# Second halves of three units' down products in three rounded passes, at the end of a recurrent-gated mixture-of-experts kernel

## Chip, cores, metric

The kernel runs on one core of a Trainium2 chip. The metric is the device time of one execution in microseconds, the median of the runs timed.

## What is computed

The input `x` is (32, 32, 128) float32. A tanh recurrence runs over 32 steps, its output goes through an RMS norm and a mixture of 16 experts with 4 chosen for each token, and `x`, the recurrence's output and the experts' sum are added. Cut to what matters:

```python
xw = jnp.einsum('ntd,dh->nth', x, Wx) + b
next_h = jnp.tanh(xw_t + prev_h @ Wh)          # 32 steps
...
xn = xf * jax.lax.rsqrt(jnp.mean(xf * xf, axis=-1, keepdims=True) + EPS) * norm_scale
vals, idx = jax.lax.top_k(xn @ wg + bg, K)     # 4 of 16
gate_full = jnp.einsum('tke,tk->te', one_hot(idx), softmax(vals))
h = jnp.einsum('th,ehd->etd', xn, w1) + b1[:, None, :]
a = jnp.minimum(h[..., ::2], LIMIT)
b = jnp.clip(h[..., 1::2], -LIMIT, LIMIT)
s = a * jax.nn.sigmoid(ALPHA * a) * (b + 1.0)
y = jnp.einsum('eti,eih->eth', s, w2) + b2[:, None, :]
t = jnp.einsum('eth,te->th', y, gate_full)     # every expert, weighted by its gate
return x + (xf + t)
```

## The kernel before

There are 1024 tokens, 8 tiles of 128. They are worked in three chunks of 2, 2 and 4 tiles. A **unit** is 512 columns of work: two experts on 256 tokens in chunks 0 and 1 (units 0 to 7 and 8 to 15), one expert on 512 tokens in chunk 2 (units 16 to 31). For each unit:

- the **up**: PE forms `a` in bank psA and `b` in psB (`up`, L913). Each is three rounded passes: weights and tokens are held as a high part rounded to the type float32r and a low part that is the rest (`w1_hi`, `w1_lo`, `xn_hi`, `xn_lo`), and the passes are high by high, low by high, high by low;
- ACT applies its two functions to psA (L586, L598), DVE clips psB into `lin` (L792) and multiplies the two into `act` (L810);
- the **gate product** `actg` = `act` times the gates laid out over the partitions (`gate_cols`). POOL makes it (L461), but for units 20, 22, 24, 26, 28 and 30 (`DVE_PRODUCT`), where DVE does (L816), and unit 31, where DVE makes it in two halves of 256 columns (L833);
- the **down**: PE adds `w2` times `actg` into the sum over experts. For chunk 2 the sum is two banks of 256 columns, psY (first half) and psM (second half).

The down has two forms. For units 0 to 15 and 28 to 31 it takes the float32 tensors `w2_sb` and `actg` as they are (L957, L969). For units 16 to 27 (`SPLIT`) it takes three rounded passes (L948), for which ACT makes `act_hi` (L550) and POOL `act_lo` (L470) of each `actg`, and earlier ACT `w2_hi` (L558) and POOL `w2_lo` (L477).

Each engine has its own program, written out by hand as a loop over units, with semaphores between them. The down of a unit comes six units after its up (`LAG`), and POOL's product three behind (`POOL_LAG`). After the last up PE runs the downs of units 26 and 27, then the float32 halves of units 28 to 31 into psY, then those into psM; these four units have no rounded parts. DVE adds `xT` to each finished bank (L840), and SP and ACT store the result (L344): the second bank in two halves of 64 partitions, one from each queue. What the end looks like on PE:

```python
for u in rest:            # 28, 29, 30, 31
    down_half(u, 0)       # psY
for u in rest:
    down_half(u, 1)       # psM
```

`down_half` waits for the product of its unit: `wait_product` for 28 to 30, `actg_tail` at 2 (both L833) for 31.

Of the kernel before, what the change touches and what calls it, by code (L numbers as in the profile page):

```python
# [15 lines left out]
def adaln_rnn_moe_kernel(nc, wx_x, small, bg, w1, w2, b2, out):  # L16
# [45 lines left out]
    SPLIT = list(range(FIRST, NU - 4))  # L62
    SPLIT_RUNS = [[u for u in SPLIT if u // 4 == k] for k in sorted({u // 4 for u in SPLIT})]
    W2_HIGH, W2_LOW = [13, 14, 17], [16, 17, 18]
    SPLIT_DEPTH = 3
    DVE_PRODUCT = list(range(FIRST + 4, NU, 2))

# [18 lines left out]
    with ctx:  # L86
        def sb(name, shape, dt=F32):
            return ctx.enter_context(nc.sbuf_tensor(name, shape, dt))
# [4 lines left out]
        def sem(name):  # L93
            return ctx.enter_context(nc.semaphore(name))
# [57 lines left out]
        actg = sb("actg", [P, SUM_DEPTH, W])  # L152
        act_hi = sb("act_hi", [P, SPLIT_DEPTH, W], F32R)
        act_lo = sb("act_lo", [P, SPLIT_DEPTH, W], F32R)
        w2_hi = sb("w2_hi", [P, len(SPLIT), H], F32R)
        w2_lo = sb("w2_lo", [P, len(SPLIT), H], F32R)
        yT = sb("yT", [P, NT * P])

        psA = [pb("psA0"), pb("psA1")]
        psB = [pb("psB0"), pb("psB1")]  # L160
# [53 lines left out]
        act_lo_ready = sem("act_lo_ready")  # L214
        w2_hi_ready = sem("w2_hi_ready")
        w2_lo_ready = sem("w2_lo_ready")
        yT_ready = sem("yT_ready")
        stored = sem("stored")
        dve_chain = sem("dve_chain")
# [110 lines left out]
        def at(table, v):  # L330
            return [k for k, w in enumerate(table) if w is not None and w == v]
# [53 lines left out]
        def _(pool):  # L385
# [101 lines left out]
            for v in range(NU - 1 + POOL_LAG):  # L487
                for q in at(RSTD, v - 1):
                    xn_low(pair_group(q))
                for q in at(POWER, v):  # L490
                    power_rstd(pair_group(q))
                for q in at(RSTD, v):
                    power_expo(q)
                    place_expo(q)
                for i in at(W2_LOW, v):
                    w2_low(i)
                if v >= POOL_LAG and v - POOL_LAG not in DVE_PRODUCT:
                    gate_product(v - POOL_LAG)
                for u in SPLIT:
                    if split_slot(u) == v:  # L500
                        act_low(u)
                for q in at(GATES, v - 1):
                    add_residuals(q)

        @block.scalar
        def _(acte):

            acte.dma_start(small_h[:, 0:SM], small).then_inc(small_loaded, 16)
            acte.dma_start(b2_sb[:, :], b2).then_inc(b2_loaded, 16)
            acte.wait_ge(ident_ready, 1)  # L510
            nc.scalar.activation(act[:, 0, 0:1], zeros[:, 0:1], ACT.Gelu_apprx_sigmoid)

            def tanh(t):
                acte.wait_ge(step_mm, t + 1)
                nc.scalar.activation(hT[:, (t + 1) * N:(t + 2) * N], step_psum(t), ACT.Tanh,
                                     bias=b_col[:, 0:1]).then_inc(step_done, 1)

            def w1_high(k):

                p, a = k // 2, k % 2  # L520
                pe_ = slice(2 * p, 2 * p + 2)
                acte.wait_ge(w1_loaded[2 * p // EG], 16)
                nc.scalar.activation(w1_hi[:, pe_, a, :], w1_sb[:, pe_, a, :], ACT.Copy).then_inc(w1_hi_ready, 1)

            def square(g):

                acte.wait_ge(step_done, TL * GROUP0[g + 1])
                nc.scalar.activation(sq[:, group_cols(g)], hT[:, group_cols(g, N)], ACT.Square).then_inc(sq_ready, 1)

            def scale_gates(q):  # L530
                acte.wait_ge(inv_ready, q + 1)
                for j in pair_tiles(q):
                    last = nc.scalar.activation(
                        gates_w[:, j, :].rearrange("p (a b e) -> p a b e", a=3, b=2)[:, :, 0, :],
                        gate_sum[:, j, :].rearrange("p (a e) -> p a e", a=1).to_broadcast([P, 3, E]),
                        ACT.Copy, scale=inv[:, j:j + 1])
                last.then_inc(scale_done, 1)

            def copy_gates(q):
                acte.wait_ge(gates_mm, q + 1)  # L540
                qc = slice(q * PW, (q + 1) * PW)
                nc.scalar.activation(gT[:, qc], psX[0:E, 0:PW], ACT.Copy).then_inc(gT_ready, 1)

            def act_high(u):

                i = SPLIT.index(u)
                wait_product(acte, u)
                if i >= SPLIT_DEPTH:
                    acte.wait_ge(y_mm, SPLIT[i - SPLIT_DEPTH] + 1)
                nc.scalar.activation(act_hi[:, i % SPLIT_DEPTH, :], actg[:, u % SUM_DEPTH, :],  # L550
                                     ACT.Copy).then_inc(act_hi_ready, 1)

            def w2_high(i):

                to, es = w2_run(i)
                for g in range(NG):
                    acte.wait_ge(w2_loaded[g], 16)
                nc.scalar.activation(w2_hi[:, to, :], w2_sb[:, es, :], ACT.Copy).then_inc(w2_hi_ready, 1)  # L558

            acte.wait_ge(small_loaded, 16)  # L560
            for t in range(HEAD):
                tanh(t)
                if t == TL:
                    square(0)
                elif t == HEAD - 1:
                    square(1)
                elif t >= W1_AT:
                    w1_high(2 * W1_DVE + t - W1_AT)
            acte.wait_ge(consts_ready, 1)
            for k in range(2 * W1_DVE + HEAD - 1 - W1_AT, 2 * NP):  # L570
                w1_high(k)
            for u in range(NU):
                c, e0, r = unit(u)
                for k in SPLIT:
                    if split_slot(k) == u:
                        act_high(k)
                if u == 0:
                    acte.wait_ge(b1_ready, 1)

                acte.wait_ge(a_mm, u + 1)  # L580
                for k in range(r):
                    if k == 1 and u < LAG:
                        for t in steps_at(u, 0):
                            tanh(t)
                    o = part(c, k)
                    last = nc.scalar.activation(psA[u % 2][:, o], psA[u % 2][:, o], ACT.Relu, scale=-1.0,  # L586
                                                bias=lim_b1a[:, e0 + k:e0 + k + 1])
                last.then_inc(relu_done, 1)
                if u >= LAG:
                    for t in steps_at(u, 0):  # L590
                        tanh(t)

                for q in range(1, NQ):
                    if GATES[q] + 1 == u:
                        scale_gates(q)
                acte.wait_ge(relu_done, u + 1)
                w = width(u)
                nc.scalar.activation(psA[u % 2][:, 0:w], psA[u % 2][:, 0:w], ACT.Gelu_apprx_sigmoid, scale=-1.0,  # L598
                                     bias=limit_col[:, :]).then_inc(swish_done, 1)
                for t in steps_at(u, 1):  # L600
                    tanh(t)
                if u == GATES[0]:
                    scale_gates(0)
                for q in at(GATES_T, u):
                    copy_gates(q)
                if u == LAST_T:
                    copy_gates(NQ - 1)
                for q in at(STATS, u + 1):
                    square(pair_group(q))
                for i in at(W2_HIGH, u):  # L610
                    w2_high(i)
            acte.wait_ge(yT_ready, NC + 1)
            store(acte, slice((NT - 2) * P, NT * P), slice(P // 2, P))

        @block.vector
        def _(dve):
# [163 lines left out]
            for v in range(NU):  # L780
# [38 lines left out]
                    gates_halves(q)  # L819
                if v == LAST_T + 1:  # L820
                    gates_halves(NQ - 1)
                for q in at(RSTD, v):
                    route_logits(q)
                    route_top(q)
                    route_index(q)
                    route_float(q)
                    route_hot(q)
# [4 lines left out]
            for o in pieces(u):  # L832
                nc.vector.tensor_tensor(by_pair(actg[:, u % SUM_DEPTH, o]), by_pair(act[:, u % ACT_DEPTH, o]), gate_block(u, o),  # L833
                                        ALU.mult).then_inc(actg_tail, 1)
            dve.wait_ge(xh_ready, NQ)
            for k in range(2):
                dve.wait_ge(y_done, k + 1)
# [5 lines left out]
        def _(pe):  # L843
# [117 lines left out]
            def down_half(u, k):  # L961
# [9 lines left out]
                if u == NU - 1:  # L971
                    ins.then_inc(y_done, 1)

            keep_warm(WARM_START)
            x_wx(0, 1)
            pe.wait_ge(small_loaded, 16)
# [60 lines left out]
            rest = range(SPLIT[-1] + 1, NU)  # L1037
            for u in range(NU - LAG, rest.start):
                down(u)
            for u in rest:  # L1040
                down_half(u, 0)
            for u in rest:
                down_half(u, 1)


# [29 lines left out]
```

## Time and profile before

| what | value |
|---|---|
| median of 3 runs | 103.24 us (103.24 to 103.46) |
| the profiled execution's own time | 102.98 us |
| its span, first to last instruction | 100.9 us |
| granted TensorE clock over the span | 1.00 of full speed |
| PE busy | 95.8 us, 95% of the span |
| DVE, ACT, POOL busy | 73.0, 69.5, 73.1 us |

The span is what the trace shows; the time of an execution holds some 2 us more around it. Times in rows are microseconds from the start of the span. PE is TensorE's matmuls, PEld its weight loads, DVE is VectorE, ACT ScalarE, POOL GpSimd, SP SyncE. A float32 matmul of 256 columns stands as two records, a rounded one as one. Records on one engine overlap, so the distance between two starts tells more than the length of one. `w_sb` in a row is `w1_sb` or `w2_sb`, `w_hi` and `w_lo` the parts of either.

### The profile page before, as it was taken

Reading aid. Unit: us, or ns where it says so; the run is one execution under the profiler, and the core shown is the slowest. Engines: PE = TensorE matmul, PEld = TensorE weight load, DVE = VectorE, ACT = ScalarE, POOL = GpSimd, SP = SyncE. Lnnn points to the kernel's source line nnn. Section 1 sums busy time; section 2 is a strip of 40 time slices with the busy share of each in tenths; the row PEclk is TensorE's granted clock in tenths of the full one; section 3 lists DMA queues with packets and bytes.
Section 4 is the critical chain, followed back from the end, with each engine's and each line's share of the span. In section 5 each row is a group of like instructions: output and inputs, shape, how many; then the busy total and the mean of one; then the engine's idle time right before and its main releaser. Section 6 shows DMA issues by size and latency. Waiting matters only on the chain.

```text
span 100.9 us, 1849 instructions
## 1 busy us (share of the span) xinstructions
PE 95.8 (95%) x589; PEld 82.0 (81%) x590; DVE 73.0 (72%) x187; ACT 69.5 (69%) x158; POOL 73.1 (73%) x83
## 2 busy tenths in 40 slices
PE   6999999999999999999999899999999999999970
PEld 2666678799999899999999688888878888889750
DVE  0306699689599785995879987669796977969630
ACT  3335997989685956769388668668887898996000
POOL 6001239993769993499817999999999999899400
PEclk9999999999999999999999999999999999999999
DMA  2998960017920009950499004992100000000012
GB/s 53 237 328 282 408 236 0 6 47 302 375 120 0 6 7 226 387 223 7 133 340 351 15 4 121 305 365 95 48 7 0 6 0 0 0 0 0 6 52 52
DMA packets 5001, 12.99 MB, mean 129 GB/s; under 512 B 752, under 2 KB 1792, under 8 KB 4992
## 3 DMA queue, kind: packets, MB, share of 16 engines
q1 hardware_dynamic: 4672, 12.66, 36.4%
q10 hardware_dynamic: 320, 0.21, 0.8%
q8 instruction: 5, 0.08, 0.3%
q14 instruction: 4, 0.03, 0.1%
HBM read 12.28 MB, written 0.59 MB: 128 GB/s over the span
## 4 chain that ended last, share of the span: by engine, by line
PE 31%; POOL 30%; DVE 11%; issue 10%; DMA 7%; ACT 4%; POOLq 2%; SPq 2%; DVEq 0%
POOL actg L461 15%; POOL act_lo L470 10%; PE psA L913 8%; DMA w_sb<-in_w 7%; PE psB L913 7%; PE psY L957 5%; POOL w_lo L477 3%; DVE lin L792 2%; POOLq L86 2%; PE psM L969 2%; PE psY L858 2%; PE psR L858 2%; PE psY L969 2%; PE psM L874 1%; DVE act L810 1%
## 5 line engine op out<-in xcount | busy, mean ns | idle before, releaser
L792 DVE TENSOR_SCALAR lin<-psB,one_b1b 128x256 f32<-128x256 f32 (+1 forms) x48 | 25.9, 568 | 11.2 <-PE psB L913 10.9
L586 ACT ACTIVATE psA<-psA,lim_b1a 128x256 f32<-128x256 f32 (+1 forms) x48 | 23.9, 515 | 11.6 <-PE psA L913 11.6
L461 POOL TENSOR_TENSOR actg<-act,gate_cols 128x512 f32<-128x512 f32 x25 | 31.9, 1289 | 0.0
L598 ACT ACTIVATE psA<-psA,limit_col 128x512 f32<-128x512 f32 x32 | 21.1, 659 | 0.8
L810 DVE SCALAR_TENSOR_TENSOR act<-lin,psA 128x512 f32<-128x512 f32 x26 | 17.8, 686 | 1.7 <-ACT psA L598 0.6
L913 PE MATMUL psA<-xn_hi,w_hi 128*128 128x256 f32 (+1 forms) x48 | 18.0, 376 | 0.4 <-DVE act L810 0.3
L913 PE MATMUL psB<-xn_hi,w_hi 128*128 128x256 f32 (+1 forms) x48 | 15.8, 330 | 0.0
L470 POOL TENSOR_TENSOR act_lo<-actg,act_hi 128x512 fp32r<-128x512 f32 x12 | 15.4, 1300 | 0.4 <-ACT act_hi L550 0.4
L913 PE MATMUL psB<-xn_lo,w_hi 128*128 128x256 f32 (+1 forms) x48 | 15.3, 318 | 0.0
L913 PE MATMUL psB<-xn_hi,w_lo 128*128 128x256 f32 (+1 forms) x48 | 15.3, 318 | 0.0
L913 PE MATMUL psA<-xn_hi,w_lo 128*128 128x256 f32 (+1 forms) x48 | 15.3, 319 | 0.0
L913 PE MATMUL psA<-xn_lo,w_hi 128*128 128x256 f32 (+1 forms) x48 | 15.1, 318 | 0.0
L414 POOL TENSOR_TENSOR rstd<-meansq,neg_half 128x2 f32<-128x2 f32 (+1 forms) x5 | 3.3, 655 | 11.6 <-DVE meansq L633 8.9
L422 POOL TENSOR_TENSOR expo<-euler,diff 128x6 f32<-128x6 f32 x4 | 5.3, 1329 | 8.1 <-DVE diff L687 8.1
L913 PEld LDWEIGHTS psA<-xn_hi,w_hi 128*128 128x128 f32 x48 | 9.1, 190 | 1.4 <-issue 1.2
L913 PEld LDWEIGHTS psB<-xn_hi,w_hi 128*128 128x128 f32 x48 | 9.1, 189 | 0.7
L913 PEld LDWEIGHTS psB<-xn_lo,w_hi 128*128 128x128 f32 x48 | 9.1, 189 | 0.7
L913 PEld LDWEIGHTS psB<-xn_hi,w_lo 128*128 128x128 f32 x48 | 9.1, 190 | 0.6
L913 PEld LDWEIGHTS psA<-xn_lo,w_hi 128*128 128x128 f32 x48 | 8.9, 188 | 0.7
L913 PEld LDWEIGHTS psA<-xn_hi,w_lo 128*128 128x128 f32 x48 | 9.1, 190 | 0.2
L957 PE MATMUL psY<-actg,w_sb 128*128 128x256 f32 x32 | 8.7, 395 | 0.0
L957 PE MATMUL psR<-actg,w_sb 128*128 128x256 f32 x32 | 8.2, 379 | 0.0
(112 smaller groups left out, 190.4 us busy)
## 6 DMA issues: line engine op xcount, KB each, us to landing
gate_cols<-gate_rows SPq DMA_DIRECT2D x16, 512.0 KB, 5.5
w_sb<-in_w SPq DMA_DIRECT2D x4, 512.0 KB, 7.5
w_sb<-in_w SPq DMA_DIRECT2D x4, 256.0 KB, 8.6
out<-yT SPq DMA_DIRECT2D x3, 128.0 KB, 1.7
wx_x_sb<-in_wx_x SPq DMA_DIRECT2D x1, 320.0 KB, 4.7
wx_x_sb<-in_wx_x SPq DMA_DIRECT2D x2, 128.0 KB, 2.6
small_h<-in_small ACTq DMA_DIRECT2D x1, 105.0 KB, 2.7
gate_rows<-gT SPq DMA_DIRECT2D x4, 16.0 KB, 1.5
```

The source lines that it names most:

```text
L414: nc.gpsimd.tensor_tensor(rstd[:, ts.start:ts.stop], meansq[:, ts.start:ts.stop], neg_half[:, :].to_broadcast([P, len(ts)]), ALU.pow).then ...
L422: nc.gpsimd.tensor_tensor(expo[:, tq, 1:K], euler[:, :, :], diff[:, tq, 1:K], ALU.pow).then_inc(pool_chain, 1)
L461: nc.gpsimd.tensor_tensor(by_pair(actg[:, u % SUM_DEPTH, w]), by_pair(act[:, u % ACT_DEPTH, w]), gate_block(u, w), ALU.mult).then_inc(actg ...
L470: nc.gpsimd.tensor_tensor(act_lo[:, i % SPLIT_DEPTH, :], actg[:, u % SUM_DEPTH, :], act_hi[:, i % SPLIT_DEPTH, :].bitcast(F32), ALU.subtra ...
L586: last = nc.scalar.activation(psA[u % 2][:, o], psA[u % 2][:, o], ACT.Relu, scale=-1.0, bias=lim_b1a[:, e0 + k:e0 + k + 1])
L598: nc.scalar.activation(psA[u % 2][:, 0:w], psA[u % 2][:, 0:w], ACT.Gelu_apprx_sigmoid, scale=-1.0, bias=limit_col[:, :]).then_inc(swish_do ...
L792: last = nc.vector.tensor_scalar(lin[:, v % 2, o], psB[v % 2][:, o], one_b1b[:, e0 + k:e0 + k + 1], LIMIT + 1.0, ALU.add, ALU.min)
L810: nc.vector.scalar_tensor_tensor(to, lin[:, v % 2, 0:w], 1.0 - LIMIT, psA[v % 2][:, 0:w], ALU.max, ALU.mult).then_inc(act_done, 1)
L858: nc.tensor.matmul(step_psum(t), wh_sb, hT[:, t * N:(t + 1) * N], start=False, stop=True, skip_group_check=True).then_inc(step_mm, 1)
L913: last = nc.tensor.matmul(bank[:, part(c, k)], w[:, e0 + k, a, :], x_part[:, cols(c)], start=((k, m) in first), stop=((k, m) in end))
L957: last = nc.tensor.matmul(y, w2_sb[:, e0 + k, :], actg[:, u % SUM_DEPTH, a], start=False, stop=(e0 + k == E - 1))
L969: ins = nc.tensor.matmul(y, w2_sb[:, e0, :], actg[:, u % SUM_DEPTH, o], start=False, stop=(u == NU - 1))
```

## The change

For units 28, 29 and 30 the second half of the down (256 columns, into psM) is made of three rounded passes in place of one float32 matmul. This needs:

- the high and low parts of `w2` for these three experts: one ACT copy of 384 columns behind unit 18's second function, and one DVE subtraction of 384 columns behind unit 19's product (`W2_TAIL_HIGH`, `W2_TAIL_LOW`);
- the high parts of the second halves of `actg`: three ACT copies of 256 columns after unit 31's functions (`tail_high`), in the order 28, 30, 29;
- their low parts: two POOL subtractions of 256 columns (28 and 30) after its last product, and one DVE subtraction (29) after unit 31's two products.

The parts of `actg` lie in the first six experts' place of `w1_lo`, which unit 21's up was the last to read. `yT` now lies in `sq`. PE takes the first halves in the order 28, 30, 29, 31, then nine rounded passes (`down_tail`), then unit 31's second half in float32.

```diff
+    TAIL_FIRST = SPLIT[-1] + 1
+    TAIL = [TAIL_FIRST, TAIL_FIRST + 2, TAIL_FIRST + 1]
+    TAIL_TO = slice(len(SPLIT), len(SPLIT) + len(TAIL))
+    TAIL_FROM = slice(TAIL_FIRST - FIRST, NU - 1 - FIRST)
+    W2_TAIL_HIGH, W2_TAIL_LOW = 18, 19
...
-        w2_hi = sb("w2_hi", [P, len(SPLIT), H], F32R)
-        w2_lo = sb("w2_lo", [P, len(SPLIT), H], F32R)
-        yT = sb("yT", [P, NT * P])
+        w2_hi = sb("w2_hi", [P, len(SPLIT) + len(TAIL), H], F32R)
+        w2_lo = sb("w2_lo", [P, len(SPLIT) + len(TAIL), H], F32R)
+        tail_hi = w1_lo[:, 0:len(TAIL), :, :].rearrange("p e a f -> p e (a f)")
+        tail_lo = w1_lo[:, len(TAIL):2 * len(TAIL), :, :].rearrange("p e a f -> p e (a f)")
+        yT = sq
...
@@ POOL, after the loop over units
+            for i in range(len(TAIL) - 1):
+                pool.wait_ge(tail_hi_ready, i + 1)
+                nc.gpsimd.tensor_tensor(tail_lo[:, i, :], actg[:, TAIL[i] % SUM_DEPTH, PW:W],
+                                        tail_hi[:, i, :].bitcast(F32), ALU.subtract).then_inc(tail_lo_ready, 1)
...
@@ ACT
+            def tail_high(u):
+
+                wait_product(acte, u)
+                nc.scalar.activation(tail_hi[:, TAIL.index(u), :], actg[:, u % SUM_DEPTH, PW:W],
+                                     ACT.Copy).then_inc(tail_hi_ready, 1)
...
+                if u == W2_TAIL_HIGH:
+                    nc.scalar.activation(w2_hi[:, TAIL_TO, :], w2_sb[:, TAIL_FROM, :], ACT.Copy).then_inc(w2_tail_hi, 1)
+            acte.wait_ge(b_mm, FIRST + 2 * len(TAIL))
+            for u in TAIL:
+                tail_high(u)
...
@@ DVE, in the loop, and after unit 31's two products
+                if v == W2_TAIL_LOW:
+                    dve.wait_ge(w2_tail_hi, 1)
+                    nc.vector.tensor_tensor(w2_lo[:, TAIL_TO, :], w2_sb[:, TAIL_FROM, :], w2_hi[:, TAIL_TO, :].bitcast(F32),
+                                            ALU.subtract).then_inc(w2_tail_ready, 1)
...
+            i = len(TAIL) - 1
+            dve.wait_ge(tail_hi_ready, i + 1)
+            nc.vector.tensor_tensor(tail_lo[:, i, :], actg[:, TAIL[i] % SUM_DEPTH, PW:W],
+                                    tail_hi[:, i, :].bitcast(F32), ALU.subtract).then_inc(tail_last_ready, 1)
...
@@ PE
+            def down_tail():
+
+                o, y = y_end(1)
+                pe.wait_ge(w2_tail_ready, 1)
+                for m, (w, x_part) in enumerate(((w2_hi, tail_hi), (w2_lo, tail_hi), (w2_hi, tail_lo))):
+                    for i in range(len(TAIL)):
+                        if m == 0:
+                            pe.wait_ge(tail_hi_ready, i + 1)
+                        elif m == 2 and i < len(TAIL) - 1:
+                            pe.wait_ge(tail_lo_ready, i + 1)
+                        elif m == 2:
+                            pe.wait_ge(tail_last_ready, 1)
+                        k = len(SPLIT) + TAIL[i] - TAIL_FIRST
+                        nc.tensor.matmul(y, w[:, k, :], x_part[:, i, :], start=False, stop=False)
...
-            for u in rest:
+            for u in TAIL + [NU - 1]:
                 down_half(u, 0)
-            for u in rest:
-                down_half(u, 1)
+            down_tail()
+            down_half(NU - 1, 1)
```

The end of PE's program before, from the first half of unit 28's down (`w_sb` is `w2_sb`, and the last word names the semaphore waited for):

```order
477 L969 MATMUL psY<-actg,w_sb 128x256 [waits actg_dve]
478 L969 MATMUL psY<-actg,w_sb 128x256 [waits actg_done]
479 L969 MATMUL psY<-actg,w_sb 128x256 [waits actg_dve]
480 L969 MATMUL psY<-actg,w_sb 128x256 [waits actg_tail]
481 L969 MATMUL psM<-actg,w_sb 128x256 [waits actg_dve]
482 L969 MATMUL psM<-actg,w_sb 128x256 [waits actg_done]
483 L969 MATMUL psM<-actg,w_sb 128x256 [waits actg_dve]
484 L969 MATMUL psM<-actg,w_sb 128x256 [waits actg_tail]
```

And with the change (`w_lo` here is the place that holds `tail_hi` and `tail_lo`):

```order
477 L1004 MATMUL psY<-actg,w_sb 128x256 [waits actg_dve] x2
478 L1004 MATMUL psY<-actg,w_sb 128x256 [waits actg_done]
479 L1004 MATMUL psY<-actg,w_sb 128x256 [waits actg_tail]
480 L1022 MATMUL psM<-w_lo,w_hi 128x256 [waits tail_hi_ready,w2_tail_ready]
481 L1022 MATMUL psM<-w_lo,w_hi 128x256 [waits tail_hi_ready] x2
482 L1022 MATMUL psM<-w_lo 128x256 x3
483 L1022 MATMUL psM<-w_lo,w_hi 128x256 [waits tail_lo_ready] x2
484 L1022 MATMUL psM<-w_lo,w_hi 128x256 [waits tail_last_ready]
485 L1004 MATMUL psM<-actg,w_sb 128x256 [waits actg_tail]
```

Unit 30's first half now stands ahead of unit 29's, and nine rounded matmuls with waits for new parts stand where three float32 ones did.

DVE's program around unit 19's product (row 140) with the change; before, row 142 followed row 140 at once:

```order
139 L819 TENSOR_SCALAR lin<-psB,one_b1b 128x512 [waits b_mm]
140 L837 SCALAR_TENSOR_TENSOR act<-lin,psA 128x512 [waits actg_done,swish_done,lin_done]
141 L851 TENSOR_TENSOR w_lo<-w_sb,w_hi 128x384 [waits w2_tail_hi]
142 L819 TENSOR_SCALAR lin<-psB,one_b1b 128x512 [waits b_mm]
143 L837 SCALAR_TENSOR_TENSOR psX<-lin,psA 128x512 [waits swish_done,lin_done]
```

One subtraction with both inputs in SBUF has come in ahead of unit 20's clip.

DVE's end with the change; the subtraction at 175 is new:

```order
172 L837 SCALAR_TENSOR_TENSOR act<-lin,psA 128x512 [waits actg_done,swish_done,lin_done]
173 L864 TENSOR_TENSOR actg<-act,gate_cols 128x256 [waits cols_loaded3_3,y_mm,cols_loaded2_3,act_done]
174 L864 TENSOR_TENSOR actg<-act,gate_cols 128x256
175 L868 TENSOR_TENSOR w_lo<-actg,w_lo 128x256 [waits tail_hi_ready]
176 L875 TENSOR_TENSOR sq<-wx_x_sb,psY 128x256 [waits y_done,xh_ready]
177 L875 TENSOR_TENSOR sq<-wx_x_sb,psM 128x256 [waits y_done]
```

Between unit 31's products and the two last additions DVE now has the low part of unit 29.

## Rows read from the trace of the kernel before

**Rows 1.** Busy time by stretch; the first line names the columns.

```profile
core 0: us, PE busy (x) PEld busy (x) DVE busy (x) ACT busy (x) POOL busy (x), PEclk, DMA share, GB/s
...
75.20:93.70 18.50, 18.50 (x110) 16.46 (x111) 15.02 (x23) 15.49 (x26) 18.12 (x15) 1.00 0.00 1
93.75:97.70 3.95, 3.88 (x18) 2.77 (x16) 1.63 (x3) 0.00 (x0) 0.59 (x1) 1.00 0.11 33
```

**Rows 2.** The chain that ended last, in order of time: start, us, what.

```profile
93.09 1.26 POOL actg L461
...
94.39 1.56 PE psY L969 x6
...
97.72 0.42 DVE yT L840
```

**Rows 3.** Timeline of PE and its weight loads at the end.

```profile
93.51 0.28 PE L948 MATMUL psY<-act_lo,w_hi 128*128 128x256 f32 x1
93.63 0.28 PE L948 MATMUL psM<-act_lo,w_hi 128*128 128x256 f32 x1
...
93.75 0.59 PE L969 MATMUL psY<-actg,w_sb 128*128 128x256 f32 x2
...
94.39 0.19 PEld L969 LDWEIGHTS psY<-actg,w_sb 128*128 128x128 f32 x1 [0.45 <-POOL actg L461]
...
94.71 0.59 PE L969 MATMUL psY<-actg,w_sb 128*128 128x256 f32 x2
...
97.30 0.38 PE L969 MATMUL psM<-actg,w_sb 128*128 128x256 f32 x1
```

**Rows 4.** Timeline of DVE from 93 us.

```profile
93.50 1.12 DVE L833 TENSOR_TENSOR actg<-act,gate_cols 128x256 f32<-128x256 f32 x1
...
94.55 0.41 DVE L833 TENSOR_TENSOR actg<-act,gate_cols 128x256 f32<-128x256 f32 x1
...
97.72 0.42 DVE L840 TENSOR_TENSOR yT<-wx_x_sb,psM 128x256 f32<-128x256 f32 x1 [1.24 <-PE psM L969]
```

**Rows 5.** Timeline of POOL, stretch 66 to 94 us.

```profile
66.38 5.01 POOL L461 TENSOR_TENSOR actg<-act,gate_cols 128x512 f32<-128x512 f32 x4
71.35 1.29 POOL L470 TENSOR_TENSOR act_lo<-actg,act_hi 128x512 fp32r<-128x512 f32 x1
...
73.85 2.54 POOL L470 TENSOR_TENSOR act_lo<-actg,act_hi 128x512 fp32r<-128x512 f32 x2
...
86.78 1.29 POOL L470 TENSOR_TENSOR act_lo<-actg,act_hi 128x512 fp32r<-128x512 f32 x1 [0.38 <-ACT act_hi L550]
...
93.04 1.30 POOL L461 TENSOR_TENSOR actg<-act,gate_cols 128x512 f32<-128x512 f32 x1
```

**Rows 6.** Timeline of PE's weight loads, two stretches.

```profile
72.73 0.19 PEld L948 LDWEIGHTS psY<-act_lo,w_hi 128*128 128x128 f32 x1
...
75.19 0.19 PEld L948 LDWEIGHTS psY<-act_lo,w_hi 128*128 128x128 f32 x1 [0.30 <-POOL act_lo L470]
```

**Rows 7.** Timeline of DVE, stretch 66 to 68 us.

```profile
66.39 0.69 DVE L810 SCALAR_TENSOR_TENSOR act<-lin,psA 128x512 f32<-128x512 f32 x1
67.84 0.75 DVE L792 TENSOR_SCALAR lin<-psB,one_b1b 128x512 f32<-128x512 f32 x1 [0.77 <-PE psB L913]
```

**Rows 8.** Groups by form: busy us, mean ns of one | idle before.

```profile
L444 POOL TENSOR_TENSOR w_lo<-w_sb,w_hi 128x256 fp32r<-128x256 f32 x10 | 6.9, 738 | 0.0
...
L523 ACT ACTIVATE w_hi<-w_sb 128x256 fp32r<-128x256 f32 x12 | 4.0, 403 | 0.4 <-DMA w_sb<-in_w 0.4
```

**Rows 9.** Timeline of POOL and DVE near 15 us.

```profile
14.32 1.33 POOL L422 TENSOR_TENSOR expo<-euler,diff 128x6 f32<-128x6 f32 x1 [1.80 <-DVE diff L687]
...
14.99 0.69 DVE L746 TENSOR_TENSOR w_lo<-w_sb,w_hi 128x512 fp32r<-128x512 f32 x1
```

**Rows 10.** Timeline of ACT, at 65 us and at its last function.

```profile
64.92 0.66 ACT L586 ACTIVATE psA<-psA,lim_b1a 128x512 f32<-128x512 f32 x1 [0.90 <-PE psA L913]
...
91.80 0.66 ACT L598 ACTIVATE psA<-psA,limit_col 128x512 f32<-128x512 f32 x1
```

More of the change, by code:

```diff
@@ L216, in adaln_rnn_moe_kernel @@
         w2_lo_ready = sem("w2_lo_ready")
+        w2_tail_ready = sem("w2_tail_ready")
+        w2_tail_hi = sem("w2_tail_hi")
+        tail_hi_ready = sem("tail_hi_ready")
+        tail_lo_ready = sem("tail_lo_ready")
+        tail_last_ready = sem("tail_last_ready")
         yT_ready = sem("yT_ready")
```

## The prediction, as put on record before the changed kernel ran

> **What bounds the kernel now.** I read the table by stretch first. From 75.2 to 93.7 us PE is busy 18.50 of 18.50 us at full clock while POOL is busy 18.12 [rows 1]: PE sets the pace, and POOL is so close behind that a delay there may reach PE. The chain that ended last comes next. It runs from POOL's product of unit 29 to PE's psY, then psM, then DVE's last addition [rows 2]. The reader is to see three things in the rows of the end. The three-pass downs step by 0.12 us per matmul (93.51, 93.63, 93.75), and a float32 matmul of 256 columns is two records 0.21 us apart, so 0.43 [rows 3]. PE does not run dense there: unit 28's first half starts at 93.75, unit 29's weights load only at 94.39 after 0.45 us idle, for POOL's product that started at 93.04 and took 1.30 [rows 3, 5]. And DVE's first product of unit 31 took 1.12 us where the second, of the same form, took 0.41; it ended at 94.62, which is 0.28 after POOL's product ended at 94.34 [rows 4, 5]. That row decides most of what follows: a DVE operation with both inputs in SBUF stood still until POOL's, which also reads SBUF, was over.
>
> The Trainium skill, "SBUF — State Buffer", section "Who interferes with whom", states this as a rule: a DVE instruction with two SBUF inputs and a GpSimd instruction that reads SBUF share a port, and who starts first has it for the whole instruction. By that rule the 1.12 us row agrees. Another row does not show it in full: DVE's 512-column subtraction at 14.99 took 0.69 us though all but its end lay inside a POOL power that started at 14.32 and took 1.33 [rows 9]. That POOL instruction reads six elements a partition, so I take it that the hold lasts as long as POOL reads, and that a long POOL product holds nearly throughout.
>
> **Part 1, PE's end.** Removed: three float32 halves, 3 x 0.43 = 1.28 us. Added: nine rounded passes, 9 x 0.12 = 1.08 us. Gain 0.20 us, all on the path. The new order of the first halves lets unit 30's down (0.43) run while unit 29's product is finished. Before, the last psM record starts at 97.30; eight float32 matmuls laid end to end from 93.75 would put it at 93.75 + 15 x 0.213 = 96.95. So 0.35 us of standing still is there to win. With both, DVE's last addition would start 0.55 us sooner than 97.72 [rows 3, 4]. That is the most that the end can give.
>
> **Part 2, what unit 31 waits for.** PE's last first-half needs both of DVE's products of unit 31. Before, the second ran at 94.55 to 94.96 because POOL had nothing left. Now POOL has two subtractions of 256 columns waiting, whose high parts ACT has long made: ACT's last function ends at 92.46 [rows 10], a 256-column copy takes 0.40 [rows 8], so units 28 and 30 are ready near 93.3. DVE's first product gets its turn at 94.34 and is over at 94.62, as before. Then POOL has been waiting and DVE's second asks at 94.55. I take it that they alternate: POOL works 0.69 us (ten such took 6.9 us [rows 8]) to near 95.27, and DVE's second product ends 0.28 after, at 95.55 instead of 94.96. After a release PE needs 0.59 us until the next matmul can start: unit 29's product ended at 94.34, its two records ended the stall, and the next matmul's record is near 94.93, 0.22 behind the one at 94.71 [rows 3]. So the rounded passes start at 95.55 + 0.59 = 96.14. The low parts are no second wait: POOL's second is done near 96.2, DVE's of unit 29 near 96.5 (ACT's copy of 29 is ready at 94.8), and the third round of passes begins at 96.14 + 6 x 0.12 = 96.86. Nine passes end at 97.22, unit 31's second record starts at 97.43, and DVE's addition, 0.42 after the last record as in the trace, starts at 97.85. Against 97.72 that is **+0.13 us**: the second product's delay has eaten 0.20 and 0.35 and a little more.
>
> **Part 3, DVE's low part of w2 at 67 us.** DVE's product of unit 19 ends at 67.08, and DVE is then idle 0.77 us until 67.84 [rows 7]. A 384-column subtraction would last some 0.55 us, between the 0.41 of 256 columns and the 0.69 of 512 [rows 4, 9]; it would fit. But POOL is in one of four products back to back (66.38, 5.01 us together, one each 1.25 [rows 5]). By the 1.12 us row DVE's subtraction stands until 67.65 and ends 0.28 x 384/256 = 0.42 later, near 68.1. Unit 20's clip starts 0.25 us late; DVE has idle time behind it and PE is two units of psB ahead, so I cost that at nothing. What counts is POOL. While DVE reads, POOL's next product can't. Two 256-column operations take 2 x 0.69 = 1.38 us, one of 512 takes 1.25, so 0.13 us of each is a fixed part that can lie under DVE's reading: POOL loses 0.42 - 0.13 = **0.29 us**. The bounds are 0 (POOL goes on unhindered) and 0.55 (the whole subtraction). POOL has no slack there to absorb it: `act_lo` of unit 16 started at 71.35, took 1.29, and PE's load of it stands at 72.73, 0.09 us later; for unit 17 PE waited 0.30 us already, until 75.19 [rows 5, 6]. From there to 93.75 PE is dense and gives nothing back, and POOL's one pause, 0.38 us at 86.78, was a wait for ACT, which follows PE [rows 1, 5]. So 0.29 us on POOL is 0.29 us at the end.
>
> The Trainium skill, "SBUF — State Buffer", section "A bandwidth-pool intuition that's wrong (but worth ruling out)", puts the loser's restart at about 115 ns after the DVE operation's end. By it POOL would lose about 0.42 + 0.1 = 0.5 us, and the sum below would be some 0.2 higher; no row of this case shows that restart.
>
> **Free parts.** ACT's copy of `w2` lies behind unit 18's second function, where ACT is idle 0.90 us before 64.92 [rows 10]; at most 1.5 x 0.40 = 0.60 us, it fits; without that cover it would delay unit 19's first function by its length. ACT's three copies at the end come after its last function, when it had nothing left but a store. `yT` in `sq` and the parts in `w1_lo` move no work: both places were last used long before. The DMAs are the same, in the same order; each store follows its addition.
>
> **Sum.** +0.29 (POOL at 67 us) + 0.13 (the end) = +0.42 us. The profiled execution took 102.98, so it would be 103.40; the median of the runs stands 0.26 above the profiled execution, so against 103.24 I forecast 103.66, say **103.7 us**. What a measurement can tell from no change is about 0.3%, 0.31 us.
>
> **The rivals.**
> - DVE's two products of unit 31 keep the port between them. For it: the second starts at 94.55, before the first has ended, so POOL may find no gap. Then the second product ends at 94.96 as before, rounded passes start at 95.54, POOL's low parts are ready near 95.6 and 96.6, since DVE's of unit 29 goes between them, which holds the eighth pass from 96.38 to about 96.6. The last addition starts near 97.5, 0.23 sooner. With 0.29 lost at 67 us: +0.06, 103.3. Chance 0.25.
> - POOL loses nothing at 67 us, because the turn to DVE falls into time that POOL does not read. Then only the end counts, -0.23 to +0.13: 103.0 to 103.4, say 103.2. Chance 0.15.
> - The other side: the port costs nothing at either place, the long DVE row being a matter of that one product. Decided by whether DVE's second product of unit 31 takes 0.41 us beside a busy POOL. Then the end gives its full 0.55: 102.7, faster. Against it is the 1.12 us row. Chance 0.13.
> - POOL always goes first while it has work. DVE's subtraction would stand from 67.08 through POOL's queue; PE's up of unit 22 needs unit 20's product, so PE stops, and POOL runs on to the low part of unit 17, at 75.1. About 7.5 us late on DVE, some 6.5 on PE: 110. For it: in the trace nothing stood behind the product that DVE waited for. Chance 0.05.
> - The rounded passes are not cheaper than float32 at this place, since weights must be loaded for nine matmuls. Against it: 93.51 to 93.75 shows 0.12 each with loads. It would add at most 0.2; chance 0.02.
>
> **How the numbers follow.** The forecast has chance 0.40. Slower by over 0.3%: most of the forecast's cases (0.35), the starved DVE (0.05), and a little of the others (0.03): 0.43. Faster: 0.13 and a little of the third (0.02): 0.15. The rest, 0.42, is no change. The bounds of POOL's loss, 0 to 0.55, around the end's -0.23 to +0.13 give 103.0 to 103.9; for the spread of medians I add a little on each side and take 102.8 to 104.1, which leaves out the two extreme cases (0.18).
>
> **What would show it.** DVE's new subtraction near 67 us lasting about 1.0 us and not 0.55; the POOL product behind it starting 0.3 us late, and PE's wait at 75.19 longer by as much. At the end DVE's second product of unit 31 taking about 1.0 us with a POOL subtraction ahead of it; a gap in PE of some 0.5 us before that unit's first half; nine passes 0.12 us apart. I am wrong if POOL's back-to-back starts at 66 to 72 us keep their 1.25 us, or if DVE's three last operations stay at 0.41 each.

## The result and the profile after

The change makes the kernel a little slower: 103.86 us median of all 22 executions against 103.34 for the kernel before in the same series. The ratio is 1.006 with a 95% interval of 1.0039 to 1.0081, so 0.4 to 0.8 us. Forecast were +0.42 us and 103.7. Every kernel here, that of before too, has some executions of 105 us and more, which the ratios leave out; the profiles of e3, e7 and e9 were taken in such ones, with 4.2 to 5.0 us more ahead of POOL's four products near 66 us, so that of these three only what follows is read.

| | before | after |
|---|---|---|
| the profiled execution | 102.98 us | 103.85 us |
| span | 100.9 us | 101.7 us |
| first cast of w1 on DVE starts (its load has landed) | 8.26 | 8.69 |
| **head**: from there to POOL's four products | 58.12 us | 58.12 us |
| **middle**: from there to PE's first half of unit 28 | 27.37 us | 27.74 us |
| **end**: from there to DVE's last addition | 3.97 us | 4.03 us |

The 0.87 us between the two profiled executions come apart cleanly. 0.43 of it is the first load of w1, which landed later in this one execution. No part of the change lies ahead of it, and over the 14 profiles here that cast starts anywhere from 7.89 to 9.25, so I take the 0.43 for chance; the head behind it is alike to the hundredth. The change's own part is 0.37 in the middle and 0.06 at the end, together 0.43.

The middle first. The timelines of DVE and POOL after, near 68 us (start, us, engine line operation):

```profile
66.84 0.69 DVE L837 SCALAR_TENSOR_TENSOR act<-lin,psA 128x512 f32<-128x512 f32 x1
67.44 1.09 DVE L851 TENSOR_TENSOR w_lo<-w_sb,w_hi 128x384 fp32r<-128x384 f32 x1
68.45 0.74 DVE L819 TENSOR_SCALAR lin<-psB,one_b1b 128x512 f32<-128x512 f32 x1
...
66.81 5.36 POOL L473 TENSOR_TENSOR actg<-act,gate_cols 128x512 f32<-128x512 f32 x4
...
66.81 1.31 POOL L473 TENSOR_TENSOR actg<-act,gate_cols 128x512 f32<-128x512 f32 x1
...
68.05 1.62 POOL L473 TENSOR_TENSOR actg<-act,gate_cols 128x512 f32<-128x512 f32 x1
```

DVE's new subtraction took 1.09 us; it ended at 68.53, 0.41 after POOL's product had ended at 68.12. The product behind it took 1.62 us instead of 1.3, and the four took 5.36 together, against 5.01 in [rows 5]: POOL lost 0.35 us. PE's weight loads show where that arrived, against 72.73 and 75.19 in [rows 6]:

```profile
73.46 0.19 PEld L983 LDWEIGHTS psY<-act_lo,w_hi 128*128 128x128 f32 x1 [0.21 <-POOL act_lo L482]
75.96 0.19 PEld L983 LDWEIGHTS psY<-act_lo,w_hi 128*128 128x128 f32 x1 [0.35 <-POOL act_lo L482]
```

The load that POOL's low part of unit 17 releases stands 9.15 us behind POOL's first product; before it was 8.81. So 0.34 us was lost there, and from it to unit 28's first half PE took 18.59 us (18.56 before): nothing was given back, as in [rows 1]. Most of it shows one load earlier: ahead of unit 16's low part PE's loads now stand idle 0.21 us, where none was idle before, and ahead of unit 17's 0.35 in place of 0.30.

The end. PE, DVE and POOL after, from 93 us, single instructions out of narrow stretches of the timeline:

```profile
94.55 1.46 PE L1004 MATMUL psY<-actg,w_sb 128*128 128x256 f32 x6
96.33 0.70 PE L1004 MATMUL psY<-actg,w_sb 128*128 128x256 f32 x2 [0.33 <-DVE actg L864]
96.68 0.71 PE L1022 MATMUL psM<-w_lo,w_hi 128*128 128x256 f32 x3
97.23 0.52 PE L1022 MATMUL psM<-w_lo 128*128 128x256 f32 x3
97.58 0.52 PE L1022 MATMUL psM<-w_lo,w_hi 128*128 128x256 f32 x3
97.94 0.59 PE L1004 MATMUL psM<-actg,w_sb 128*128 128x256 f32 x2
...
94.30 1.11 DVE L864 TENSOR_TENSOR actg<-act,gate_cols 128x256 f32<-128x256 f32 x1
...
95.34 0.94 DVE L864 TENSOR_TENSOR actg<-act,gate_cols 128x256 f32<-128x256 f32 x1
...
96.20 0.94 DVE L868 TENSOR_TENSOR w_lo<-actg,w_lo 128x256 fp32r<-128x256 f32 x1
...
98.58 0.42 DVE L875 TENSOR_TENSOR sq<-wx_x_sb,psM 128x256 f32<-128x256 f32 x1 [1.02 <-PE psM L1004]
...
95.09 0.91 POOL L518 TENSOR_TENSOR w_lo<-actg,w_lo 128x256 fp32r<-128x256 f32 x1
...
95.96 0.90 POOL L518 TENSOR_TENSOR w_lo<-actg,w_lo 128x256 fp32r<-128x256 f32 x1
```

The first six psY records run without the pause of [rows 3]: unit 30 covers unit 29. Then PE waits for DVE's second product of unit 31, which took 0.94 us where it took 0.41 in [rows 4]. DVE and POOL take turns: DVE's product ends at 95.41, POOL's subtraction at 96.00, DVE's product at 96.28, POOL's at 96.86, DVE's subtraction at 97.14, and each is some 0.2 to 0.5 us longer than alone. From the second of the nine passes, near 96.99, to unit 31's record at 97.94 the starts stand 0.12 apart, as reckoned; only the first one's record, at 96.68 and 0.47 long, begins earlier, right behind PE's wait.

### The profile page after: what moved, and what is told of

Same layout as the page of the kernel before. It is cut to its first block, busy times and chain, and to the rows that moved or that the text cites. A ratio compares the mean times of both kernels' runs of the same rounds, so it can differ in the third digit from the quotient of the medians.

```text
span 101.7 us, 1866 instructions
## 1 busy us (share of the span) xinstructions
PE 95.6 (94%) x593; PEld 81.6 (80%) x593; DVE 75.2 (74%) x189; ACT 70.9 (70%) x162; POOL 75.2 (74%) x85
## 4 chain that ended last, share of the span: by engine, by line
PE 41%; POOL 18%; DVE 14%; ACT 8%; DMA 7%; issue 6%; SPq 2%; POOLq 0%; DVEq 0%
PE psA L948 12%; POOL actg L473 10%; PE psB L948 10%; DMA w_sb<-in_w 7%; PE psY L992 5%; ACT psA L608 3%; DVE lin L819 3%; POOL w_lo L489 3%; POOL act_lo L482 2%; PE psY L983 2%; DVE act L837 2%; DVE actg L864 2%; PE psM L983 2%; ACT psA L620 2%; PE psY L893 2%
```

## The experiments

The table has for each run its time against the kernel before, and the two stretches (middle, end), in us, since they hold neither the loads at the start nor what lies around the span. The expectations of e1 to e4 speak of one stretch from the first cast of w1 to the last addition; that holds the head, which is 58.1 to 58.3 us in most profiles but was 58.50 in e2. Each stretch comes from one traced execution. The nine kernels in which DVE reads no two SBUF inputs at 67 us for this subtraction agree in the middle to 0.05 us (27.37 to 27.42), and e12 with them. The times carry more scatter than that: e3 and e4 have the same stretches to 0.01 us, and their times stand at 0.9996 and 0.9945.

| run | middle | end | time against before (95%) |
|---|---|---|---|
| before | 27.37 | 3.97 | 1 |
| the change | 27.74 | 4.03 | 1.006 (1.0039 to 1.0081) |
| e1 middle alone | 27.69 | 3.97 | too few runs to compare |
| e2 order alone | 27.38 | 3.71 | 0.9968 (0.995 to 0.9986) |
| e3 w2 through PSUM | 27.40 | 4.03 | 0.9996 (0.9968 to 1.0023) |
| e4 the same, twice | 27.39 | 4.04 | 0.9945 (0.9898 to 0.9992) |
| e5 low parts on DVE | 27.72 | 3.49 | 0.9995 (0.9969 to 1.0021) |
| e6 one product waited for | 36.07 | 3.52 | 1.004 (1.001 to 1.0071) |
| e7 = e3 + e6 | 27.41 | 3.52 | 1.0019 (0.9988 to 1.005) |
| e8 = e3 + e5 + e6 | 27.39 | 3.43 | 1.0033 (1.0009 to 1.0057) |
| e9 = e3 + e5 | 27.42 | 3.49 | 0.9953 (0.9915 to 0.9991) |
| e10 = e2 + the wait of e6 | 27.38 | 3.66 | too few runs to compare |
| e11 = e8 with one wait less | 27.38 | 3.43 | 0.9988 (0.9945 to 1.003) |
| **e12** = e5, later subtraction | 27.41 | 3.50 | **0.9938** (0.9912 to 0.9964) |

### e1: the middle's work alone

```diff
@@ the kernel before: ACT behind unit 18, DVE behind unit 19
+ nc.scalar.activation(w2_hi[:, TAIL_TO, :], w2_sb[:, TAIL_FROM, :], ACT.Copy)
+ nc.vector.tensor_tensor(w2_lo[:, TAIL_TO, :], w2_sb[:, TAIL_FROM, :], w2_hi[:, TAIL_TO, :].bitcast(F32), ALU.subtract)
```

> The kernel before, with only ACT's copy and DVE's subtraction of 384 columns of w2 near 67 us added (their results are not used; yT lies in sq as in the change). I compare the stretch from DVE's first w1 cast to the start of DVE's last addition, which leaves out when the first w1 load lands: 89.46 us before, 89.89 with the change. Port theory: DVE's subtraction lasts about 1.1 us, POOL's four products 5.35 us in place of 5.01, stretch 89.8 (+0.35), time +0.3%. Rival, all of the loss lies in the end: stretch 89.46.

```profile
66.62 1.11 DVE L830 TENSOR_TENSOR w_lo<-w_sb,w_hi 128x384 fp32r<-128x384 f32 x1
...
66.03 5.33 POOL L465 TENSOR_TENSOR actg<-act,gate_cols 128x512 f32<-128x512 f32 x4
```

The subtraction took 1.11 us, POOL's four products 5.33, the middle was 27.69 (+0.32), the end 3.97; the stretch of the expectation was 97.69 - 7.89 = 89.80, as the port theory had it. The middle's loss belongs to these two instructions and needs nothing of the end.

### e2: the order of the last downs alone

```diff
-            for u in rest:
+            for u in (28, 30, 29, 31):      # both loops
```

> The kernel before, with only the order of the last downs changed to 28, 30, 29, 31 in both halves; no rounded passes. Nothing of POOL's follows its product of unit 29, so DVE's second product takes 0.41 us. If PE's standing still there was the wait for unit 29 and then for unit 31 as worked out: matmul after unit 31's first half at 0.59 after that product, last addition 0.25 us sooner against the last up, stretch 89.2. Rival, the wait for unit 31 takes the place of that for unit 29: stretch 89.4 to 89.5.

The end is 0.26 us shorter (expected 0.25), which the time shows too, 0.3%. The stretch as a whole was 89.59 and missed my 89.2, because its head was 0.38 longer. So part of what the change brought can be had without any rounded pass.

### e3 and e4: one input from PSUM

```diff
+                    nc.scalar.activation(psX[:, 0:len(TAIL) * H], w2_sb[:, TAIL_FROM, :]..., ACT.Copy)
@@ DVE, behind unit 19; in e4 twice
-   nc.vector.tensor_tensor(w2_lo[...], w2_sb[:, TAIL_FROM, :], w2_hi[...], ALU.subtract)
+   nc.vector.tensor_tensor(w2_lo[...], psX[:, 0:len(TAIL) * H], w2_hi[...], ALU.subtract)
```

> The change, with ACT also copying the three experts' w2 in float32 to PSUM (psX, free then), and DVE's subtraction of 384 columns reading that and w2_hi: one input in SBUF. Port theory: the subtraction lasts 0.55 us, POOL's four products 5.01, PE's wait for unit 17's low part is back near 0.3, stretch 89.55 against the change's 89.89. Rival, the loss comes from the work itself and not from its input in SBUF: stretch 89.9.

> As the one before, with that subtraction done twice (the first time into a place that is free), so that DVE is as late with unit 20 as in the change, about 1.1 us of work, but reads one input from PSUM. Port theory: POOL's four products 5.01 and stretch 89.55. Rival, DVE's lateness with unit 20 costs the 0.35 us: stretch 89.9.

DVE and POOL in e4:

```profile
66.91 0.55 DVE L855 TENSOR_TENSOR xn<-psX,w_hi 128x384 f32<-128x384 f32 x1
67.38 0.55 DVE L857 TENSOR_TENSOR w_lo<-psX,w_hi 128x384 fp32r<-128x384 f32 x1
...
66.28 5.03 POOL L473 TENSOR_TENSOR actg<-act,gate_cols 128x512 f32<-128x512 f32 x4
```

The same subtraction takes 0.55 us in the midst of the same POOL products, POOL's four take 5.02 and 5.03, and the middle is back at 27.40 and 27.39. In e4 DVE is busy nearly as long as in the change: its clip of unit 20 starts 1.56 us behind the start of POOL's four products, 1.64 in the change, 1.46 before. The loss is gone all the same: not DVE's lateness costs the 0.35 us, the second input in SBUF does. That e4's time stands at 0.9945 is not explained by its stretches, which are 0.09 us longer than before; it rests on four executions.

### e5: all low parts on DVE

```diff
@@ POOL: its loop over tail_lo removed; DVE, behind unit 31's products
+            for i in range(len(TAIL)):
+                dve.wait_ge(tail_hi_ready, i + 1)
+                nc.vector.tensor_tensor(tail_lo[:, i, :], actg[:, TAIL[i] % SUM_DEPTH, PW:W], tail_hi[:, i, :].bitcast(F32), ALU.subtract)
```

> The change, with all three low parts of actg made by DVE behind unit 31's products and none by POOL. I read two stretches that do not hold the loading of the weights: the middle, from the start of POOL's four products to PE's first half of unit 28 (27.37 us before, 27.74 with the change), and the end, from there to the start of DVE's last addition (3.97 before, 4.03 with the change). Port theory: DVE's two products of unit 31 take 1.45 us together as before, not 1.98, the rounded passes start 0.6 us sooner, the three low parts are done before the third round of passes, end 3.5; the middle stays 27.74. Rival, the end is held by PE's many weight loads: end 4.0.

```profile
93.86 1.44 DVE L860 TENSOR_TENSOR actg<-act,gate_cols 128x256 f32<-128x256 f32 x2
95.22 1.08 DVE L864 TENSOR_TENSOR w_lo<-actg,w_lo 128x256 fp32r<-128x256 f32 x3
```

The middle is 27.72: the loss at 67 us is untouched. With POOL quiet DVE makes both products in 1.44 us and three low parts in 1.08; in the change they were two in 1.98 and one in 0.94. The end is 3.49. Giving POOL a share of the work made both later.

### e6, e7, e8, e10, e11: PE waits for the product that it reads

```diff
-                    pe.wait_ge(actg_tail, 2)
+                    pe.wait_ge(actg_tail, k + 1)     # in e11 only at k == 0
```

> The change, with PE's first half of unit 31 waiting for one of DVE's two products of unit 31 (the one that it reads) and not for both. POOL and DVE keep their order. If what the end lost is PE's wait for the second product: PE runs the four first halves without a pause, end 3.45 to 3.6, though DVE's products still take 1.98 us together; a pause moves to the third round of passes, which needs low parts. Rival, the low parts end the stretch: end 3.9 to 4.0.

> The edit of e6 together with that of e3 (w2's subtraction reads one input from PSUM). If the two losses are apart: middle 27.39, end as in e6, 0.5 us less in all than before, time 0.995 of before.

> The edits of e3, e5 and e6 together. DVE's products take 1.45 us, low parts are ready before they are needed, PE is dense from unit 28's first half to the end: 8 records of 0.213, 9 of 0.12, one of 0.213 and 0.42 give an end of 3.42; middle 27.39; time 0.9945 of before.

> The kernel before with the order of e2 and the wait of e6, no rounded passes. In e6, e7 and e8 the time around the span was 2.7 us, in all others 2.1. If that comes with the wait edit by itself: 2.7 here too, and the time is no better than e2's though the end is shorter (16 records of 0.213 less one, and 0.42: 3.62 against e2's 3.71). Rival, it needs the rounded passes too: 2.1 and time 0.996 of before.

> As e8, but PE's second half of unit 31 has no wait of its own (DVE's last low part, for which PE has waited by then, comes behind that product on DVE). PE then has one wait instead of two for unit 31. End and middle as in e8, 3.42 and 27.39. If the additional wait is what adds 0.6 us around the span: 2.1 there, and time 0.994 of before; else 2.7 and 1.00.

The end came out as expected in all five: 3.52, 3.52, 3.43, 3.66, 3.43. e10 against e8 and e11 gives what the rounded passes bring by themselves: 3.66 to 3.43, 0.23 us (the prediction's 0.20). But the time didn't follow: expected were 0.995 of before in e7 and 0.9945 in e8, measured 1.0019 and 1.0033. In the four with rounded passes and this wait (e6, e7, e8, e11) the time of an execution around its span was 2.7 to 2.8 us in the median, and anything from 1.8 to 3.2 in single ones; in the others the median was 1.9 to 2.1. e11 has one wait less than e8 and the same 2.7; e10 has the wait without rounded passes and 2.1 in all six of its executions. So neither the wait nor the passes bring it alone, and what these 0.6 us are stays open; no row of a trace holds them.

e6 showed something else. Its profiled execution, of 111.5 us, was this:

```profile
67.23 8.48 DVE L851 TENSOR_TENSOR w_lo<-w_sb,w_hi 128x384 fp32r<-128x384 f32 x1
...
66.62 5.02 POOL L473 TENSOR_TENSOR actg<-act,gate_cols 128x512 f32<-128x512 f32 x4
71.57 1.29 POOL L482 TENSOR_TENSOR act_lo<-actg,act_hi 128x512 fp32r<-128x512 f32 x1
72.79 1.29 POOL L473 TENSOR_TENSOR actg<-act,gate_cols 128x512 f32<-128x512 f32 x1
74.01 1.29 POOL L482 TENSOR_TENSOR act_lo<-actg,act_hi 128x512 fp32r<-128x512 f32 x1
...
77.16 0.79 PE L948 MATMUL psA<-xn_hi,w_hi 128*128 128x512 f32 x1 [6.01 <-DVE psX L837]
```

DVE's subtraction stood 8.48 us: it asked during the first of POOL's four products, POOL went on through six more operations at its usual steps, and DVE got its turn only when POOL, fed by DVE through PE and ACT, had run dry at 75.30. PE stood 6.0 us. What PE's clock did, in the columns of [rows 1] (PEclk is the third figure from the end):

```profile
71.00:75.00 4.00, 0.14 (x1) 0.00 (x0) 4.00 (x1) 0.61 (x2) 4.00 (x4) 1.00 0.00 0
77.00:81.00 4.00, 3.85 (x12) 3.27 (x13) 3.31 (x7) 1.87 (x3) 0.18 (x1) 0.50 0.12 37
84.00:92.00 8.00, 8.00 (x48) 7.01 (x47) 6.56 (x10) 6.97 (x12) 5.58 (x5) 1.00 0.00 0
```

When PE started again behind these 6.0 us, its clock was 0.50 of full, 1.2 GHz and not 2.4, and 512-column passes stood 0.43 apart instead of 0.23; from 84 us it was full again.

DVE had asked 0.61 us into a POOL product. In the executions in which it got in after one product it asked at 0.63 (the change), 0.59 (e1) and 0.57 (e5). So the moment of asking, as far as these rows tell, doesn't decide it; what does stays open.

### e9 and e12: both losses removed

```diff
-    W2_TAIL_HIGH, W2_TAIL_LOW = 18, 19
+    W2_TAIL_HIGH, W2_TAIL_LOW = 18, 27       # e12, with the edit of e5
```

> The edits of e3 and e5 together, without that of e6: w2's subtraction reads one input from PSUM, and DVE makes all three low parts of actg. If both losses are the shared port: middle 27.39, end 3.49 (as measured in e3 and e5), 0.46 us less than before in the two stretches, and time 0.9955 of before, since the time around the span was 2.1 us in e3 and e5.

> The edit of e5, with DVE's subtraction of w2 behind unit 27's product in place of unit 19's, both inputs in SBUF as in the change. DVE then asks for the port near 84.9 us on the clock of before, inside a POOL product, ahead of POOL's pause of 0.38 us at 86.4. Port theory with the slack that the prediction names: the subtraction still lasts about 0.9 to 1.1 us and POOL's next operation is late by about 0.3, but the pause takes it up: middle 27.4, end 3.5, time 0.9955 of before. Rival, a late POOL costs its 0.3 us wherever it is: middle 27.7.

Both are faster than the kernel before, e9 by 0.5% and e12 by 0.6%. What the scatter of the times leaves open, the stretches bear out: in both kernels the two together are 0.43 us shorter, 0.4%. e12's DVE and POOL:

```profile
84.98 0.77 DVE L847 TENSOR_TENSOR w_lo<-w_sb,w_hi 128x384 fp32r<-128x384 f32 x1
...
85.28 1.63 POOL L482 TENSOR_TENSOR act_lo<-actg,act_hi 128x512 fp32r<-128x512 f32 x1
```

POOL's operation behind the subtraction takes 1.63 us and not 1.3, as in the change, but the middle is 27.41: the pause that POOL had ahead of 86.78 [rows 5] takes it up, and POOL's operation behind the pause starts 20.45 us behind the four products' start, 20.40 before. The same loss costs 0.35 us at 67 us and nothing at 85.

## Why the prediction was right

- **POOL at 67 us, +0.29.** Right in mechanism, and 0.06 to 0.08 too small: POOL lost 0.35, the middle 0.37 (0.32 in e1). The subtraction ended 0.41 behind POOL's product (0.42 reckoned). What failed is the 0.13 us of a POOL operation that I let lie under DVE's reading; the rows give 0.06. The other price for it, about 0.5 us, did not come out.
- **No slack between POOL and PE there.** Right: the loss stood whole at PE's load at 75.96, and none of it came back. The sign named for it was not: PE's wait at that load was to be some 0.3 longer and was 0.05 longer (0.35 against 0.30). The prediction's own rows had unit 16's load only 0.09 behind POOL, so the loss was due there first, and there PE stood 0.21.
- **The end, +0.13.** Right in mechanism, 0.07 too large. DVE's second product ended 1.73 us behind PE's start of unit 28, not 1.80; from its end to the last addition it is 2.30, as reckoned (0.59 + 1.08 + 0.21 + 0.42). That the two take turns was a choice and not worked out from a row; the rows show the turns.
- **The most that the end can give, 0.55.** e8 and e11 reached 0.54, with PE's wait changed.
- **Sum.** +0.42 forecast, +0.43 in the two stretches of the profile, 0.4 to 0.8 in the series. That the first two agree to the hundredth is luck: the middle was forecast 0.08 too small and the end 0.07 too large.
- **Rivals.** That DVE keeps the port for both products: no, it was 0.94. That POOL loses nothing, and that the port costs nothing: fell with e1 and e3. That rounded passes cost as much: fell with e10 against e8.
- **POOL always first, chance 0.05, 110 us.** Not what the median shows, but it exists: e6's profile is that case (PE 6.0 us idle against 6.5, POOL at work until 75.30 against 75.1, 111.5 us against 110). Its middle is 8.7 us longer than before, 2.7 more than PE's idle time; the rows behind it show passes at half clock, which I hadn't reckoned. In the four kernels with both inputs in SBUF at 67 us (the change, e1, e5, e6) 6 of 54 executions had a span over 107 us, at 108.0 to 112.5; in the 89 executions of the kernel before whose span is on record and 101 of the other nine kernels, none had one over 106.1. Only e6's trace shows the cause; for the other five it is inferred.
- **Who has the port.** The Trainium skill, "SBUF — State Buffer", section "Who interferes with whom", has the first to start hold the port for its whole instruction. The turns at the end and e3 agree, but for the 0.06 us by which POOL lost less than the 0.41 of DVE's work behind it. Who follows when both have work queued is seen in the rows alone: DVE after one operation in the change, e1, e5 and e12, and in e6 only after seven. So it need not be the one that waits.

## What to carry to other kernels

Before work is put on DVE beside a busy GpSimd, look whether both inputs lie in SBUF; if so, it costs GpSimd time (0.32 to 0.35 us here for 384 columns), and the place decides whether that is free: put it where the other engine has a pause ahead of its next due time, or read one input from PSUM. Two engines that share a port are not two engines: at the end here one alone made three low parts and two products sooner than both together (2.20 us behind PE's start of unit 28 in e5, 2.59 in the change). And a subtraction that waits for a port may, now and then, wait for the whole queue of the other, as traced once here; look at the longest executions too, not at the median alone.

## What was not expected

- DVE's 384-column subtraction lasted 0.55 us with one input from PSUM. With both in SBUF and POOL working it lasted 0.77 behind unit 27's product and 1.09 to 1.13 behind unit 19's, and once, from that same place, 8.48.
- The time around the span differs between near-alike kernels: 1.9 to 2.1 us in ten of them, 2.7 to 2.8 in the four that have both the rounded passes and the wait of e6.
